# Moving the sums of weight blocks from VectorE to GpSimd in a three-pass fp32 mixture-of-experts kernel

## The reference

```python
xg = xf[dispatch]                                     # 8 experts, 97 tokens each
gate = silu(einsum("ech,ehi->eci", xg, rg))           # routed: inner width 4096
up   = einsum("ech,ehi->eci", xg, ru)
eout = einsum("eci,eih->ech", gate * up, rd)
...
shared = silu(x @ sg) * (x @ su) @ sd                 # all tokens, inner width 8192
return shared + routed
```

## Time and profile before

| | |
|---|---|
| median of 3 runs | 2847.54 us (2847.41 to 2847.99) |
| the profiled execution's own time | 2846.59 us |
| its span, from first to last instruction | 2845.0 us |
| TensorE busy | 2817.0 us (99%) |
| VectorE busy | 2230.6 us (78%) |
| ScalarE busy | 1489.6 us (52%) |
| GpSimd busy | 57.3 us (2%) |
| granted TensorE clock, mean | 0.997 |

### The profile page before, as it was taken

How to read it: one execution, slowest core, us unless ns; L and a number is a source line. 1 busy time by engine, 2 the same in 40 slices (tenths; PEclk the granted TensorE clock), 3 DMA queues, 4 the chain that set the end, 5 groups by cost and what they waited for, 6 DMA issues and landing times.

```text
span 2845.0 us, 42616 instructions
## 1 busy us (share of the span) xinstructions
PE 2817.0 (99%) x15886; PEld 2371.4 (83%) x15886; DVE 2230.6 (78%) x2728; ACT 1489.6 (52%) x1941; POOL 57.3 (2%) x73
## 2 busy tenths in 40 slices
PE   9999999999999999999999999999999999999999
PEld 8996998788888888888888888888888888888877
DVE  8846255888888888888888888888888888888888
ACT  7722222565555555555555555555555555555563
POOL 0010000000000000000000000000000000000001
PEclk9999999999999999999999999999999999999999
DMA  4110131476666666666666666666666666666676
GB/s 113 38 60 30 60 104 44 146 268 218 216 222 216 215 218 223 216 214 215 226 217 217 219 227 218 217 218 226 216 219 218 231 222 219 216 223 221 222 259 234
DMA packets 270284, 549.19 MB, mean 193 GB/s; under 512 B 16674, under 2 KB 82466, under 8 KB 269928
## 3 DMA queue, kind: packets, MB, share of 16 engines
q1 hardware_dynamic: 265954, 532.11, 55.3%
q0 software_dynamic: 3936, 14.06, 1.6%
q10 hardware_dynamic: 162, 0.08, 0.0%
HBM read 537.49 MB, written 8.70 MB: 192 GB/s over the span
## 4 chain that ended last, share of the span: by engine, by line
PE 94%; DVE 4%; issue 1%; ACT 0%; DMA 0%; DVEq 0%; SPq 0%; ACTq 0%
PE ps L1853 26%; PE ps L1857 26%; PE ps L1856 26%; PE ps L1625 3%; PE ps L1666 3%; PE ps L1665 3%; PE ps L1664 3%; PE ps L1714 2%; DVE c_lo L1412 1%; PE ps L1904 1%; PE ps L1750 1%; PE ps L1748 1%; PE ps L1749 1%; PE ps L1758 0%; DVE oh_d L990 0%
## 5 line engine op out<-in xcount | busy, mean ns | idle before, releaser
L1412 DVE TENSOR_TENSOR c_lo<-raw,c_hi 128x1024 fp32r<-128x1024 f32 x832 | 985.2, 1219 | 101.8 <-ACT c_hi L795 101.4
L795 ACT CAST c_hi<-raw 128x1024 fp32r<-128x1024 f32 x832 | 862.9, 1050 | 169.2 <-PE ps L1857 153.9
L1853 PE MATMUL ps<-tok_hi,c_hi 128*128 128x314 f32 x1792 | 552.9, 309 | 1.0 <-DVEq L1601 0.6
L1856 PE MATMUL ps<-tok_lo,c_hi 128*128 128x314 f32 x1792 | 551.8, 308 | 0.0
L1857 PE MATMUL ps<-tok_hi,c_lo 128*128 128x314 f32 x1792 | 551.8, 308 | 0.0
L1853 PE MATMUL ps<-c_hi,xgT_hi 128*97 128x512 f32 x1024 | 404.1, 395 | 2.9 <-DVE xgT_lo L1471 2.9
L1857 PE MATMUL ps<-c_hi,xgT_lo 128*97 128x512 f32 x1024 | 403.9, 394 | 0.0
L1856 PE MATMUL ps<-c_lo,xgT_hi 128*97 128x512 f32 x1024 | 402.9, 394 | 0.0
L1478 DVE TENSOR_TENSOR resid<-ps,resid 125x512 f32<-125x512 f32 x320 | 218.9, 686 | 178.3 <-PE ps L1857 178.2
L1853 PEld LDWEIGHTS ps<-tok_hi,c_hi 128*128 128x128 f32 x1792 | 339.4, 189 | 4.1 <-issue 1.0
L1856 PEld LDWEIGHTS ps<-tok_lo,c_hi 128*128 128x128 f32 x1792 | 339.7, 190 | 1.4
(11 more groups left out here) (249 smaller groups left out, 3875.9 us busy)
## 6 DMA issues: line engine op xcount, KB each, us to landing
raw<-in_L_ffn_rg SPq DMA_DIRECT2D x256, 512.0 KB, 4.7
raw<-in_L_ffn_ru SPq DMA_DIRECT2D x256, 512.0 KB, 4.7
raw<-in_L_ffn_rd SPq DMA_DIRECT2D x256, 512.0 KB, 6.0
raw<-in_L_ffn_sg SPq DMA_DIRECT2D x64, 512.0 KB, 5.4
raw<-in_L_ffn_su SPq DMA_DIRECT2D x64, 512.0 KB, 5.5
raw<-in_L_ffn_sd SPq DMA_DIRECT2D x64, 512.0 KB, 5.4
wl<-in_L_mix_w_qkv SPq DMA_DIRECT2D x6, 2048.0 KB, 8.2
wl<-in_L_gnn_W SPq DMA_DIRECT2D x2, 2048.0 KB, 22.9
```

What stands on the lines that cost most here:

```text
L795: nc.scalar.copy(c_hi[u % RING][:], raw_at_(q, r)[:]).then_inc(sem("hi_done"), 1 + (U - UNITS) * (u == UNITS - 1))
L1412: V.tensor_tensor(c_lo[u % RING][:], raw_at_(q, r)[:], c_hi[u % RING][:].bitcast(F32), ALU.subtract).then_inc(sem("lo_done"), 1 + (U - UNI ...
L1853: m = MM(out_, l_hi, r_hi, start=first, stop=False, skip_group_check=skip)
L1856: MM(out_, l_hi, r_lo, start=False, stop=False, skip_group_check=skip)
```

## The change

The four sums of steps 1 to 30 are issued on GpSimd, in `factor_sums(e, q)`, with the same operands, the same buffers and the same counts on `sums` for ScalarE to wait on. Steps 0 and 31 keep them on VectorE. GpSimd's loop over experts is written out, so that counts and addresses are constants, and the `turns` counts in it are gone.

```diff
+        def factor_sums(e, q):
+            b11, b21, b22, b12 = [STEP.b0 + r for r in (R_A11, R_A21, R_A22, R_A12)]
+            ra, rc, rd_, rb = [raw_at_(q, b)[:] for b in (b11, b21, b22, b12)]
+            for b in (b11, b21):
+                pool.wait_ge(raw_sem(q, b), raw_full(e, q, b))
+            nc.gpsimd.tensor_tensor(rc, ra, rc, ALU.subtract).then_inc(sem("sums"), 1)
+            pool.wait_ge(raw_sem(q, b22), raw_full(e, q, b22))
+            pool.wait_ge(sem("lo_done"), count(e, q, U, U + STEP.at(F_S3) + 1))
+            nc.gpsimd.tensor_tensor(rc, rd_, rc, ALU.subtract).then_inc(sem("sums"), 1)
+            pool.wait_ge(sem("sums"), count(e, q, 4, SUM_BEFORE[F_S2]))
+            nc.gpsimd.tensor_tensor(ra, rc, ra, ALU.add).then_inc(sem("sums"), 1)
+            pool.wait_ge(raw_sem(q, b12), raw_full(e, q, b12))
+            pool.wait_ge(sem("lo_done"), count(e, q, U, U + STEP.at(F_A12) + 1))
+            nc.gpsimd.tensor_tensor(rb, rb, rc, ALU.subtract).then_inc(sem("sums"), 1)
 ...
         def turn_over(e):
-            pool.dma_start(eout_d[bass.ds(e * CAP, CAP), :], eout[:]).then_inc(sem("eout_stored"), 16)
+            pool.dma_start(eout_d[e * CAP:(e + 1) * CAP, :], eout[:]).then_inc(sem("eout_stored"), 16)
 ...
-        with pool.Fori(0, E - 1) as e:
-            turn_over(e)
-
-            pool.wait_ge(sem("t_done"), e * (2 * Q) + 2 * Q)
-            pool.sem_inc(sem("turns"), 1)
-            nc.gpsimd.tensor_copy(tok_cur[0:CAP, :], tok_u[:, bass.ds(e + 1, 1)]).then_inc(sem("tok_copied"), 1)
-            pool.wait_ge(sem("tok_copied"), e + 1)
-            pool.sem_inc(sem("turns"), 1)
-            gather()
-        turn_over(E - 1)
+        for e in range(E):
+            if e:
+                factor_sums(e, 0)
+            turn_over(e)
+            for q in range(1, Q if e < E - 1 else Q - 1):
+                factor_sums(e, q)
+            if e < E - 1:
+                pool.wait_ge(sem("t_done"), e * (2 * Q) + 2 * Q)
+                nc.gpsimd.tensor_copy(tok_cur[0:CAP, :], tok_u[:, e + 1:e + 2]).then_inc(sem("tok_copied"), 1)
+                pool.wait_ge(sem("tok_copied"), e + 1)
+                gather()
 ...
             def sums(i):
-                factor_sum(e, q, order, i)
+                if order is LAST:
+                    factor_sum(e, q, order, i)
```

## The result

| | before | after |
|---|---|---|
| median | 2847.76 us | 2904.57 us |
| all runs | 2847.41 to 2848.33, 4 runs | 2902.42 to 2906.81, 4 runs |
| profiled execution, span | 2846.59, 2845.0 | 2904.54, 2902.8 |

The ratio is 1.0198, 95% interval [1.0185, 1.0211]: 57 us slower. The prediction was 2904.5. Of the runs further down, one of the four executions of e4_no_s4 took 3089.41 us at a granted clock of 0.847 and is left out of its ratio.

A forecast was written before the change was run, and what follows sets the result against it. TensorE's own work was taken to bound steps 1 to 30. Stalls of 51 us plus 6 for late first steps made 57 on 2846.6: 2903.6, with the median 0.9 higher, 2904.5 us; range 2872 to 2940.

The forecast's parts named there:

- TensorE sets the time, and VectorE's 147 us are worth nothing: Steps 1 to 30: TensorE idles only 0.34 us, so removing 147 us of sums from VectorE gains nothing.
- GpSimd and VectorE block each other for a whole instruction: Sums beside low parts (c_lo): the second to issue waits until the first ends; full blocking, 2904 us, chance 0.60.
- whoever waits goes first: When a GpSimd or VectorE instruction ends, the other engine's waiting instruction runs next; no size of its own.
- First stall 1.15, second 0.55: TensorE waits each step: 1.15 us at unit 2 (sum S1 blocks lo2), 0.55 at unit 5 (sum S4 blocks lo5).
- Late first steps, 6 us: First steps of experts 2 to 6: lo1 comes late at ScalarE's loop turn, slack no longer covers it, 6 us.
- GpSimd's written-out loop costs nothing: GpSimd's loop branches, `turns` counts and dynamic addresses vanish on a nearly idle engine: worth nothing.
- Sum S3: nothing, at most 0.3 a step: Sum S3 over the shared down projection: taken as 0, upper bound 0.3 us a step, 9 us; 0 where q = 0.
- No fall of the clock: TensorE's granted clock was not expected to go under 1.00 in these steps because of its new pauses.
- no blocking: Rival: GpSimd and VectorE run side by side, only the five late steps stall, 5 us: 2852 us; chance 0.08.
- Sum S4 before lo4: Rival, heavier case: sum S4 goes ahead of lo4, second stall 1.4 instead of 0.55, 25 us more: 2930; chance 0.20.

The follow-up runs named there:

- e4_no_s4: The changed kernel with sum S4 given back to VectorE, sums S3, S2 and S1 on GpSimd: 2899.09 us, 1.0178 to the kernel before.
- the halves: The changed kernel with each GpSimd sum made as two instructions of 512 columns: 2932.84 us, 1.0298 to the kernel before.
- e12_before_act_out: The kernel before with nothing but ScalarE's loop over experts written out: 2846.98 us, 1.0001 to the kernel before.
- e1_loop_only: The changed kernel with all four sums back on VectorE, GpSimd's loop still written out: 2858.12 us, 1.0038 to the kernel before.
- e8_s1_s4: The changed kernel with only sums S1 and S4 on GpSimd, S3 and S2 on VectorE: 2900.47 us, 1.0186 to the kernel before.
- e9_gather_later: e1_loop_only plus ten counts on an unused semaphore around the copy ahead of the gather, to delay it: 2850.94 us, 1.0015 to the kernel before.
- e2_s3: The changed kernel with only sum S3 on GpSimd, the others back on VectorE: 2850.22 us, 1.0009 to the kernel before.

## Why the prediction was right, point by point

- **TensorE sets the time, and VectorE's 147 us are worth nothing.** Right: sum S3 alone on GpSimd gives nothing back, and no run could be told from before as faster.
- **GpSimd and VectorE block each other for a whole instruction.** Right, and shown four ways: lo2 2.32 us beside sum S1, sum S4 3.25 behind lo4, lo4 3.02 behind sum S4, and 1.22 beside clears that read nothing. That whoever waits goes first, read from one case in the earlier trace rows, held in each of the halves' turns.
- **First stall 1.15, second 0.55.** Mechanism and place right, sizes 1.06 and 0.28. A blocked `c_lo` ends about 1.08 after the sum and not 1.2, which shortens both. The second is half of what was predicted, because TensorE also comes to unit 5 0.11 later, by the late second matmul after the first stall. The prediction had no term for that: 0.11 and 0.10 a step. In all a step costs 1.57, for 1.7 predicted: 47 us in 30 steps for 51.
- **Late first steps, 6 us.** Too small. The five steps grew by 17.0 us in the profiled execution; less 5 x 1.57 that is 9.2 us. What it was worked out from held in sum: ScalarE's idle time ahead of hi0 and hi1 of these steps is 19.7 us, and was 19.0 before, though the gather had moved. It cost TensorE 4.3 us over before at unit 2, not 6. Two things that were put at 0 make up the rest: the clock, 3.4 us, and sum S3 in steps with q = 0, 1.6 us (both below). Writing out ScalarE's loop gives back 8.5 us: the clock's 3.4, these 4.3, and the 0.9 that the five steps were late before.
- **GpSimd's written-out loop costs nothing.** Wrong as a step. It costs 11 us with the sums on VectorE, where ScalarE stands 3.37 to 3.97 us ahead of hi1. In the changed kernel it is no term on top: ScalarE stands there 1.04 to 2.41 us, 7.5 in sum against 8.0 before. That the two kernels differ in this was luck for the sum.
- **Sum S3: nothing, at most 0.3 a step.** Right: nothing in the steps with q > 0. In the first steps of experts it costs 0.3 (a stall of 1.39 instead of 1.05 at experts 1 and 7), where I had said 0. With S3 alone on GpSimd one can see how: the last three low parts of the step ahead of expert 1's take 5.84 us instead of 3.50, so lo0 and lo1 end 0.36 later, which that run's slack covers. Step 1 begins 1.0 us later than before (592.03 against 590.99). That is no cost of the change: over the kept profiles it begins at 590.4 to 593.6, the last with every sum on VectorE (e12_before_act_out).
- **No fall of the clock.** Wrong in three steps, 1.1 us each.

The sum came out at the measured time because 4 us too much in the stalls stood against 3 too little in the late first steps and 1 ahead of step 1. To within a us that is luck; the 50 us of the sums (2896.10 against 2846.20, both loops written out in both) are not.

The rivals: *no blocking* is refuted by the rows of lo2 and by the runs with S1 and S4. *Sum S4 before lo4* happened where lo4 was not ready, with S1 and S4 alone on GpSimd, and gave the stall of about 1.2 at unit 4 that this order was priced by; in the change lo4 went first.

## What to carry to other kernels

Here a VectorE instruction with two SBUF inputs and a GpSimd instruction that reads SBUF did not overlap (lo2 2.32 us beside sum S1, 1.22 alone): count the GpSimd instruction's full time, here 2.40 against 1.22 us, against every VectorE instruction that comes due meanwhile, and ask which consumer that one feeds. Such work moved to an idle engine was free only where the waiting consumer had slack for the longer hold (sum S3, or S1 behind a VectorE sum S2), and cut into pieces it waited once for each piece. An edit to one engine's queue can change a delay at another engine's loop turn, so an edit that "does nothing" deserves a run of its own.

## What was not expected of the hardware

**The granted clock can fall after a pause of about 2 us.** In the changed kernel TensorE stood 2.09 us beyond its pace at unit 2 of the first step of expert 3. The windows behind it (length, then busy us of each engine, then PEclk):

```profile
1416.00:1417.00 1.00, 1.00 (x6) 1.00 (x5) 0.08 (x1) 0.00 (x0) 1.00 (x1) 0.50 0.00 0
1418.00:1419.00 1.00, 1.00 (x9) 1.00 (x9) 0.20 (x1) 0.77 (x1) 0.31 (x1) 1.00 0.91 342
```

The granted clock was 0.50, the lower of the two levels, 1.2 GHz. Matmuls stood 0.26 us apart instead of 0.145, from 1413.86 to 1417.16, so that 1.8 us of work took 3.3. The step as a whole lost 1.1, as the later stall at unit 5 was gone. It fell after pauses of 2.07, 2.09 and 3.69 us, and did not after 1.76 and 2.50, nor after the 1.05 of the common steps. The length alone doesn't decide: over the kept profiles it fell after 20 of the 30 pauses of 1.9 us or more (the shortest 1.92) and not after one of 3.35, and after none of the shorter ones. With ScalarE's loop written out no pause was over 1.4 us and no step shows it. A stall can so cost more than its length.

**ScalarE's loop turn** cost it from 0.9 to 4 us ahead of hi1, in many cases with nothing that the profile names as the wait. It was longest with sum S3 on VectorE and the gather 10.4 us ahead of unit 0: 3.37 to 3.97 us in e1_loop_only, 2.60 to 3.95 in e8_s1_s4. It was shorter with a later gather (2.07 to 2.84, e9_gather_later), and shorter with the same gather and sum S3 on GpSimd (1.04 to 1.96, e2_s3). What sets it stays open.
